# A graph network with two relational layers and two attention layers: attention rows fetched by edge tile and copied to slots by SyncE

## The chip, the cores and the metric

The kernel runs on one core of a Trainium2 chip, in one launch. The metric is the device time of that launch in microseconds (us), the median of several runs. A core has TensorE (PE, matrix products), VectorE (DVE), ScalarE (ACT), GpSimd (POOL) and SyncE (SP, which here only issues transfers), and 16 DMA engines that all of them share.

## The reference, cut to what matters

6250 nodes with 128 features, 100000 edges sorted by their target `dst`. Four layers follow one another, each over all edges: two relational ones (RGCN), then two attention ones (GAT, four heads).

```python
# setup: dst = (6250 * uniform ** 2), then edges sorted by dst
h = relu(layernorm(x))
def _rgcn_layer(h, src, dst, rel, basis, w_comp, loop_w, bias):
    W = einsum('rb,bio->rio', w_comp, basis)
    agg = segment_sum(h[src], dst * 16 + rel)          # per node and relation
    return relu(einsum('nri,rio->no', agg, W) + h @ loop_w + bias)
x = x + rgcn(rgcn(h))
h = relu(layernorm(x))
def _gat(x, src, dst, W, a_src, a_dst, b):             # self loops are added to src, dst
    xw = (x @ W).reshape(n, 4, 32)
    e = leaky_relu(al_s[src] + al_d[dst], 0.2)
    ee = exp(e - segment_max(e, dst)[dst])
    out = segment_sum(ee / den[dst] * xw[src], dst)
    return out + b
h = elu(batchnorm(gat(h))); h = elu(batchnorm(gat(h)))
out = x + h
```

## The kernel before

**Tiles, windows, slots.** The sorted edges are cut into `NG` = 782 tiles of 128 edges. The nodes are cut into 49 windows of 128. A slot is one pair of a tile and a window that it touches: `NGS` = 782 + 48 = 830 slots (832 with padding). A tile that straddles a border between windows has two slots. As `dst` is 6250 times the square of a uniform number, early windows hold many edges and late ones few: tile t lies near window 49 (t/782)^2, so borders are rare at first and come about every eighth tile at the end.

**A layer's loop.** For each slot DVE builds a selection matrix (128 edges x 128 nodes), PE multiplies it with the slot's 128 rows of source features, and DVE adds the product to the window's accumulator in SBUF (`AC`). The source rows come from a table in DRAM by an indirect DMA that POOL issues, one instruction for 128 rows.

- RGCN (`tensor`, `vector`, `scalar`; loops over `s`): POOL gathers the 782 tiles of `Ttab` (one row for each node and relation) into a ring of `TG` = 64 tiles. SP's `relay` waits for each landing and raises `landed[L]` by one. PE reads from registers which tile a slot needs (`TIX`) and where it lies (`OFT`), waits for `landed[L]` to reach that number, and multiplies.
- GAT (`gat_vector`, `gat_scalar`, `gat_tensor`): POOL gathers 830 times, once for each slot, rows of 132 floats of `Gtab` (128 features and 4 attention terms) into a ring of `GR` = 96 slots. Slots are worked in chunks of `CH` = 32. While chunk c is multiplied (L1979) and added (L1128), chunk c+1 is prepared: selections, their transposes, target terms, the maxima by scans, exponentials, and the weights are multiplied into the rows (`weigh`, L1103). In this preparation ACT's copy `als` (L1545) is the first that needs the gathered rows, of all 32 slots.
- A slot's gather in GAT waits for the gather 16 before it and, from slot 96 on, for the product that last read its place.

**Closing.** `NTURN` = 83 turns go over the windows. A turn takes a finished window, weighs it against its self loops (DVE, L588), turns it by two products (PE, L592 and L593), adds the bias (ACT, L1599) and takes statistics for the batch norm (DVE, L1213). `CLOSE` lists batches (slot from which the weights of the batch are worked out, first turn, last turn). Turns 0 to 63 are spread over the slot loop at the places in `PLACES`, the last 19 come after it.

**The start.** SP loads x, `dst` twice (to test that it is sorted), the first parameters, more of x, then `src` and `edge_type`. DVE tests the order (`flag`), PE multiplies the 49 windows by the 16 relation matrices (L1799), and SP stores `Ttab`. Between windows the generators `tables_vector`, `tables_scalar` and `tables_tensor` make the per-slot tables step by step.

Each engine runs its own instruction stream in the order written; counters (semaphores) tie them together.

## Time and profile before

| what | value |
| --- | --- |
| median of 3 runs | 5504.15 us (5494.9 to 5508.55) |
| span of the profiled execution, first to last instruction | 4547.9 us |
| median less span | 956.3 us |
| mean granted TensorE clock | 0.649 of full speed |
| busy share of the span | POOL 69%, PE 69%, DVE 56%, ACT 24% |

The profile covers the span alone; of the profiled execution nothing outside its span is shown. Shares are means over stages with different limits, so they are read by stage.

### The profile page before, as it was taken

The numbers are of one execution on the slowest core, as the hardware profiler recorded it, in microseconds if no ns is written. First come the engines' busy times: TensorE is split into PE (matmuls) and PEld (weight loads), VectorE is DVE, ScalarE is ACT, GpSimd is POOL, SyncE is SP. The second block draws the span as 40 slices with busy tenths as digits, with TensorE's granted clock in tenths as the row PEclk, the third lists the DMA queues.
The fourth block names the chain that finished last, engine by engine and source line by source line (L and its number), as shares of the span: only waits on it lengthen the run. The fifth ranks groups of instructions, "written<-read, shape, count | busy, mean of one in ns | idle before, by whom it ended". The sixth has DMA issues, their size and how long they took to land.

```text
span 4547.9 us, 63220 instructions
## 1 busy us (share of the span) xinstructions
PE 3121.2 (69%) x13439; PEld 2273.6 (50%) x13439; DVE 2544.8 (56%) x9924; ACT 1107.5 (24%) x2623; POOL 3132.4 (69%) x3271
## 2 busy tenths in 40 slices
PE   7976777777756666666646676767674666676766
PEld 3444444444434444444435555656563555565655
DVE  6534444444434455555556566767674667676776
ACT  3311222222200111111122233323332223332333
POOL 1057777777767777777677777777727777777772
PEclk9966889888855555555555566656665556665666
DMA  6633444444432222222222222222212222222222
GB/s 232 259 111 98 151 148 154 149 150 154 154 97 62 65 65 65 66 66 66 61 54 54 54 54 54 54 54 54 54 39 58 55 55 55 55 54 54 54 55 73
DMA packets 168049, 394.03 MB, mean 87 GB/s; under 512 B 57414, under 2 KB 92036, under 8 KB 150532
## 3 DMA queue, kind: packets, MB, share of 16 engines
q0 software_dynamic: 103616, 215.16, 17.9%
q10 hardware_dynamic: 37536, 102.42, 6.0%
q1 hardware_dynamic: 26532, 72.39, 4.3%
q8 instruction: 131, 2.15, 0.2%
q14 instruction: 234, 1.92, 0.1%
HBM read 229.57 MB, written 160.17 MB: 86 GB/s over the span
## 4 chain that ended last, share of the span: by engine, by line
PE 39%; DMA 15%; DVE 14%; issue 13%; POOL 11%; ACT 4%; DVEq 2%; SPq 1%; ACTq 0%; POOLq 0%
DMA Gr<-Ttab,GID 12%; PE B L1837 11%; PE B L1979 8%; POOL Gr L2098 8%; PE B L1737 6%; PE B L1799 3%; POOL Gr L2081 3%; DMA Gr<-Gtab,SRC 3%; DVE XA L1128 2%; DVE XA L935 2%; DVE Sr L1027 2%; PE B L1911 1%; PE B L1895 1%; ACT hold L1534 1%; DVE Gr L1103 1%
## 5 line engine op out<-in xcount | busy, mean ns | idle before, releaser
L2098 POOL DMA_INDIRECT Gr<-Gtab,SRC x1660 | 1603.1, 966 | 584.2 <-issue 448.5
L2081 POOL DMA_INDIRECT Gr<-Ttab,GID x1564 | 1497.3, 957 | 604.6 <-PE B L1837 272.8
L1837 PE MATMUL B<-Gr,Sr 128*128 x3328 | 999.0, 410 | 596.5 <-SPq L2114 328.6
L1837 PEld LDWEIGHTS B<-Gr,Sr 128*128 128x128 f32 x3328 | 731.3, 270 | 1051.9 <-issue 1036.4
L1979 PE MATMUL B<-Gr,Sr 128*128 128x136 f32 x3328 | 959.3, 432 | 132.9 <-DVE XA L1128 80.9
L1979 PEld LDWEIGHTS B<-Gr,Sr 128*128 128x128 f32 x3328 | 740.3, 295 | 203.7 <-DVE XA L1128 130.3
L935 DVE TENSOR_TENSOR XA<-XA,B 128x128 f32 x1664 | 471.6, 283 | 571.8 <-PE B L1837 521.3
L1128 DVE TENSOR_TENSOR XA<-XA,B 128x136 f32 x1664 | 480.8, 289 | 294.2 <-PE B L1979 237.9
L924 DVE TENSOR_SCALAR Sr<-iota,DL 128x128 f32<-128x128 f32 x1664 | 493.3, 300 | 20.6 <-issue 16.2
L1737 PE MATMUL B<-XA,H 128*128 128x512 f32 x664 | 412.5, 709 | 1.7 <-DVE H L602 0.4
L1027 DVE TENSOR_SCALAR Sr<-iota,DL 128x128 f32<-128x128 f32 x1664 | 370.2, 295 | 0.0
L1526 ACT CAST hold<-Sr 128x512 bf16<-128x512 f32 x416 | 257.2, 618 | 431.2 <-DVE Sr L1027 419.3
L1360 ACT COPY Sr<-B 128x512 f32<-128x512 f32 x332 | 194.3, 585 | 470.5 <-PE B L1737 470.5
L1895 PE MATMUL B<-identb,hold 128*128 128x128 bf16 x1664 | 232.3, 286 | 75.0 <-ACT hold L1534 48.6
L1918 PE MATMUL B<-ident,hold 128*128 128x128 f32 x52 | 23.4, 451 | 357.1 <-ACT hold L1545 357.1
L1534 ACT COPY hold<-B 128x512 bf16<-128x512 bf16 x416 | 241.7, 583 | 47.8 <-PE B L1911 45.7
L1103 DVE TENSOR_TENSOR Gr<-Gr,B 128x1024 f32<-128x1024 f32 x202 | 244.6, 1211 | 1.1 <-ACT scs L1579 1.1
L1895 PEld LDWEIGHTS B<-identb,hold 128*128 128x128 bf16 x1664 | 174.8, 132 | 117.4 <-ACT hold L1534 68.2
L1038 DVE TENSOR_TENSOR pen<-hold 128x127 f32<-128x127 f32 x52 | 15.1, 291 | 377.2 <-ACT hold L1549 377.2
L1911 PE MATMUL B<-A,hold 128*128 x1664 | 164.7, 182 | 80.5 <-ACT hold L1534 72.6
L602 DVE COPY H<-B 128x128 f32<-128x128 f32 x215 | 62.0, 289 | 270.2 <-PE B L1715 264.7
L1911 PEld LDWEIGHTS B<-A,hold 128*128 128x128 bf16 x1664 | 142.8, 113 | 123.5 <-issue 105.5
(287 smaller groups left out, 3001.2 us busy)
## 6 DMA issues: line engine op xcount, KB each, us to landing
Ttab<-Sr ACTq DMA_DIRECT2D x83, 1024.0 KB, 4.2
Ttab<-Sr SPq DMA_DIRECT2D x51, 1024.0 KB, 3.9
Gr<-Gtab,SRC POOLq DMA_INDIRECT x1660
Gr<-Ttab,GID POOLq DMA_INDIRECT x1564
Gtab<-Gr ACTq DMA_DIRECT2D x83, 66.0 KB
X1D<-Gr ACTq DMA_DIRECT2D x83, 64.0 KB
out<-Sr SPq DMA_DIRECT2D x12, 256.0 KB
Gtab<-XA SPq DMA_DIRECT2D x5, 528.0 KB, 3.8
```

The source lines that it names most:

```text
L924: e.tensor_scalar(out=selr(sn), in0=iota[:, :], scalar1=DL[:, sn:sn + 1], scalar2=None, op0=ALU.is_equal).then_inc(built_v, 1)
L935: ins = e.tensor_tensor(a, a, B[RGCN_BANKS[L][sa % len(RGCN_BANKS[L])]][:, 0:P], ALU.add)
L1027: e.tensor_scalar(out=sel(s), in0=iota[:, :], scalar1=DL[:, s:s + 1], scalar2=None, op0=ALU.is_equal).then_inc(sel_made, 1)
L1103: e.tensor_tensor(g, g, w, ALU.mult).then_inc(wei_v, 1)
L1128: ins = e.tensor_tensor(a, a, B[s % 3][:, 0:CW], ALU.add)
L1737: e.matmul(B[bk][:, :], hT[:, u % 2, :], wl[1][:, i * 512:(i + 1) * 512], start=True, stop=True).then_inc(row_mm, 1)
L1837: e.matmul(B[banks[s % len(banks)]][:, 0:P], selr(s), Gr[:, bass.ds(o, P)], start=True, stop=True).then_inc(slot_mm, 1)
L1895: mm = e.transpose(bt[:, j * P:(j + 1) * P], sbf[:, g % 2, j * P:(j + 1) * P], identb[:, :])
L1911: mm = e.matmul(B[5][:, 12 * m:12 * m + 12], sts[:, g % 2, j * P:(j + 1) * P], A3[:, bass.ds(off(e, regs[m % 16], 12 * NW), 12)], start=Tr ...
L1979: e.matmul(B[s % 3][:, 0:CW], sel(s), Gr[:, (s % GR) * CW:(s % GR + 1) * CW], start=True, stop=True).then_inc(gat_mm, 1)
L2081: e.indirect_dma_start(out=Gr[:, (sn + 1) % TG * P:((sn + 1) % TG + 1) * P], out_offset=None, in_=Tt[L][:, :], in_offset=bass.IndirectOffs ...
L2098: e.indirect_dma_start(out=Gr[:, (s % GR) * CW:(s % GR) * CW + 132], out_offset=None, in_=T2[L][0:NPAD][:, :], in_offset=bass.IndirectOffs ...
```

## The change

1. **GAT by tiles.** POOL gathers 782 tiles a layer, not 830 slots, into a new ring of 64 tiles behind `Gr`, whose slot ring shrinks from 96 to 64. POOL announces landed tiles in fours: before it issues the last tile of a four, it waits for the four before and raises `landed[2 + L]` by 4. From tile 16 on a gather waits for the copy of the slot 16 before it (`spread`).
2. **Slot copies.** SP runs `to_slots`: for each slot it waits until its tile has landed and its place is free, and copies 128 x 132 floats from the tile ring to the slot ring, SBUF to SBUF. What waited for gathers in GAT (ACT's `als`, DVE's clearing of `AC`) now waits for copies.
3. **Source table.** `SRC` is no longer selected for each slot by 28 products and two copies, but made for each tile by one shift of `GID` on DVE.
4. **A fifth batch** in `CLOSE`: turns 64 to 71 move into the slot loop, 11 stay behind it.
5. **First loads.** `dst` comes before x; `src` and `edge_type` before most of x; the later parts of x and the second basis wait until the first relation matrices have been loaded. DVE tests the order before it measures x. Tables start at window 3, not 1. Loads of 112 rows are cut into 96, 15 and 1.
6. **Landing counts.** The number that PE (and now SP) waits for is first bounded below by 1 with a register instruction.

Arrays are placed anew in SBUF to make room; the arithmetic of the layers is the same.

```diff
-GR = 96
+GR = 64
+TW = 132
+TQ = 4
+NTQ = 8
-CLOSE = ((239, 0, 17), (399, 17, 34), (558, 34, 52), (668, 52, 64))
+CLOSE = ((239, 0, 17), (399, 17, 34), (558, 34, 52), (668, 52, 64), (736, 64, 72))
+        def wait_tiles(e, L, g):
+            e.wait_ge(tiles[L][g % NTQ], 16 * TQ * (g // NTQ) + 16 * min(TQ, NG - TQ * g))
+        def wait_spread(e, n):
+            e.wait_ge(spread[n % NSG], 16 * (n // NSG + 1))
...
+            then(e.tensor_scalar(out=SRC[:, :], in0=GID[:, 0:NT], scalar1=4, scalar2=None, op0=ALU.arith_shift_right), "src")
...
-                if w >= 1 and not early:
+                if w >= LATER and not early:
...
-                for n in range(n0 + NSG, min(n0 + 2 * NSG, 2 * NG + (L + 1) * NGS)):
-                    wait_gather(e, n)
+                for n in range(end - NSG, end):
+                    wait_spread(e, n)
                 then(e.copy(v3(dc[:, 1, :]), G3(c, 128, 132).rearrange("p s h -> p h s")), "als")
...
-                        e.wait_ge(landed[L], kregs[s % 32 // 16][s % 16])
+                        e.reg_alu(kreg, kregs[s % 32 // 16][s % 16], 1, ALU.max)
+                        e.wait_ge(landed[L], kreg)
...
-                for s in range(NGS):
-                    n = 2 * NG + L * NGS + s
-                    wait_gather(e, n - NSG)
-                    if s >= GR:
-                        e.wait_ge(gat_mm, L * NS + s - GR + 1)
+                for t in range(NG):
+                    g = t // TQ
+                    if t % TQ == TQ - 1 and g:
+                        wait_tiles(e, L, g - 1)
+                        e.sem_inc(landed[2 + L], TQ)
+                    back = t - TG + NGS - NG
+                    if back >= 0:
+                        wait_spread(e, L * NGS + back)
                     e.indirect_dma_start(
-                        out=Gr[:, (s % GR) * CW:(s % GR) * CW + 132], out_offset=None, in_=T2[L][0:NPAD][:, :],
-                        in_offset=bass.IndirectOffsetOnAxis(ap=SRC[:, s:s + 1], axis=0)).then_inc(gat[n % NSG], 16)
+                        out=TILES[:, (t + 1) % TG * TW:((t + 1) % TG + 1) * TW], out_offset=None, in_=T2[L][0:NPAD][:, :],
+                        in_offset=bass.IndirectOffsetOnAxis(ap=SRC[:, t:t + 1], axis=0)).then_inc(tiles[L][g % NTQ], 16)
+                for g in range((NG + 1) // TQ - 1, -(-NG // TQ)):
+                    wait_tiles(e, L, g)
+                    e.sem_inc(landed[2 + L], TQ)
...
+        def to_slots(e, L, kreg, kregs, oregs):
+            for s in range(NGS):
+                n = L * NGS + s
+                if s % 16 == 0:
+                    e.reg_load(kregs, TIX[:, s:s + 16])
+                    e.reg_load(oregs, OFT[0:1, s:s + 16])
+                if n >= NSG:
+                    wait_spread(e, n - NSG)
+                if s >= GR:
+                    e.wait_ge(gat_mm, L * NS + s - GR + 1)
+                e.reg_alu(kreg, kregs[s % 16], 1, ALU.max)
+                e.wait_ge(landed[2 + L], kreg)
+                o = off(e, oregs[s % 16], (TG - 1) * TW)
+                e.dma_start(Gr[:, s % GR * CW:s % GR * CW + TW], TILES[:, bass.ds(o, TW)]).then_inc(spread[n % NSG], 16)
...
-            x_load(0)
             for k, (t, o) in enumerate(((fdi, 0), (fni, 1))):
                 e.wait_ge(ready, k + 1)
                 flat_load(t, "dst", o, flat_dst)
+            x_load(0)
+            for k, (t, name) in enumerate(((fsi, "src"), (fri, "edge_type_16"))):
+                e.wait_ge(ready, k + 3)
+                flat_load(t, name, 0, flat_sem)
             e.dma_start(lw[0][:, :], I["L0_gnn_loop_w1"]).then_inc(first_params, 16)
             e.dma_start(rb[0][:, :], row(I["L0_gnn_bias1"])).then_inc(first_params, 16)
+            e.wait_ge(wall_sem[0], 16)
             x_load(1)
             x_load(2)
```

POOL's queue in GAT, before: gathers of slots 94 to 97 of the first GAT layer, where the second wait comes in.

```order
L2098 DMA Gr<-Gtab,SRC 128x132 [waits gather10]
L2098 DMA Gr<-Gtab,SRC 128x132 [waits gather11]
L2098 DMA Gr<-Gtab,SRC 128x132 [waits gat_products,gather12]
L2098 DMA Gr<-Gtab,SRC 128x132 [waits gat_products,gather13]
L2098 DMA Gr<-Gtab,SRC 128x132 [waits gat_products,gather14]
```

And of the change: the first gathers of the same layer, by tile.

```order
L2122 DMA Gr<-Gtab,SRC 128x132 [waits tables_vector,rest_done]
L2122 DMA Gr<-Gtab,SRC 128x132 x6
L2122 DMA Gr<-Gtab,SRC 128x132 [waits tiles0_0]
L2122 DMA Gr<-Gtab,SRC 128x132 x3
L2122 DMA Gr<-Gtab,SRC 128x132 [waits tiles0_1]
L2122 DMA Gr<-Gtab,SRC 128x132 x3
L2122 DMA Gr<-Gtab,SRC 128x132 [waits tiles0_2]
L2122 DMA Gr<-Gtab,SRC 128x132 [waits spread0]
L2122 DMA Gr<-Gtab,SRC 128x132 [waits spread1]
L2122 DMA Gr<-Gtab,SRC 128x132 [waits spread2]
```

POOL no longer waits for products; every fourth gather waits for the four tiles before its own four, and from tile 16 on each waits for a slot copy.

SP's queue between the relational and the attention layers had nothing to do for GAT but the stores of the second table. In the change it holds three rows for each of 1660 slots; here from slot 63 of the first GAT layer, where the wait for products comes in (L2159 is the copy).

```order
L2156 REGISTER_ALU [waits spread15]
L351 ISA [waits landed2]
L2159 DMA Gr<-Gr 128x132
L2150 TENSOR_LOAD TIL
L2151 TENSOR_LOAD TIL
L2156 REGISTER_ALU [waits gat_products,spread0]
L351 ISA [waits landed2]
```

What POOL waited for before (the product that frees a place) now stands ahead of SP's copy, 64 slots back.

SP's queue at the start of the program, before.

```order
L2125 DMA XA<-in_x 128x16x128
L2121 DMA Gr<-in_dst 111x896 [waits cleared]
L2122 DMA Gr<-in_dst 1x544
L2121 DMA Gr<-in_dst 111x896 [waits cleared]
L2122 DMA Gr<-in_dst 1x543
L2130 DMA lw<-in_L_gnn_loop_w 128x128
L2131 DMA rb<-in_L_gnn_bias 128x128
L2125 DMA XA<-in_x 128x16x128 x2
```

The same place in the change.

```order
L2167 DMA Gr<-in_dst 96x896 [waits cleared]
L2168 DMA Gr<-in_dst 15x896
L2169 DMA Gr<-in_dst 1x544
...
L2169 DMA Gr<-in_dst 1x543
L2172 DMA XA<-in_x 128x16x128
...
L2180 DMA lw<-in_L_gnn_loop_w 128x128
L2181 DMA rb<-in_L_gnn_bias 128x128
L2172 DMA XA<-in_x 128x16x128 [waits wall0]
```

The first part of x moved behind `dst`, and its second and third parts behind the load of the relation matrices.

## Rows read from the trace of the kernel before

**Rows 1.** Groups by line: busy us, mean ns, then idle time before and what ended it.

```profile
L2098 POOL DMA_INDIRECT Gr<-Gtab,SRC x1660 | 1603.1, 966 | 584.2 <-issue 448.5 <-PE B L1979 122.5 <-DVEq L973 13.3
L1837 PE MATMUL B<-Gr,Sr 128*128 x3328 | 999.0, 410 | 596.5 <-SPq L2114 328.6 <-DVE XA L935 222.1 <-issue 40.5
```

**Rows 2.** Timeline of POOL: start, duration, idle before; relational, then attention layer.

```profile
261.66 0.98 POOL L2081 DMA_INDIRECT Gr<-Ttab,GID  x1 [0.30 <-issue]
...
2425.92 0.95 POOL L2098 DMA_INDIRECT Gr<-Gtab,SRC  x1 [0.30 <-issue]
```

**Rows 3.** Stretches of three layers: PE, PEld, DVE, ACT, POOL, clock, DMA share, GB/s.

```profile
400.00:1240.00 840.00, 630.97 (x2287) 378.36 (x2287) 354.68 (x1578) 209.43 (x396) 637.01 (x666) 0.86 0.44 151
...
2280.00:3320.00 1040.00, 692.53 (x3811) 583.35 (x3812) 678.38 (x2525) 315.55 (x779) 791.60 (x816) 0.59 0.21 54
3430.00:4460.00 1030.00, 694.90 (x3846) 583.29 (x3846) 680.89 (x2526) 316.89 (x783) 781.95 (x815) 0.60 0.21 55
```

**Rows 4.** Waits in a chunk with closing, 3183 to 3223 us: total, times, longest.

```profile
ACT hold L1545 <- DMA Gr<-Gtab,SRC: 7.0, 1, 7.0
```

**Rows 5.** Timeline, end of the first GAT layer's gathers and what follows.

```profile
3329.95 0.95 POOL L2098 DMA_INDIRECT Gr<-Gtab,SRC  x1 [0.30 <-issue]
3333.32 0.42 ACT L1545 COPY hold<-Gr 128x128 f32<-128x128 f32 x1 [8.08 <-DMA Gr<-Gtab,SRC]
...
3344.27 4.45 PE L1979 MATMUL B<-Gr,Sr 128*128 128x136 f32 x18
```

**Rows 6.** Transfers of 66 KB like a slot copy: issue on ACT, and time to landing.

```profile
L1399 ACTq MOVE Gtab<-Gr x83: 29/29/29, 1406.5 to 2268.9; - x83
L1399 ACTq DMA_DIRECT2D Gtab<-Gr x83: 338/338/339, 1406.6 to 2268.9; - x83
DMA to landing us min/median/max: 3.4/3.9/5.0
```

**Rows 7.** Timeline of SP at the start: issue of two loads of 1 MB of x.

```profile
12.02 14.91 SPq L2125 DMA_DIRECT2D XA<-in_x  x2
```

**Rows 8.** Timeline of DVE after the last slot of the first GAT layer: first and last of 19 turns.

```profile
3372.00 1.10 DVE L588 TENSOR_TENSOR Gr<-XA,GID 128x256 f32 x3 [0.25 <-DVE GID L1187]
...
3386.28 0.29 DVE L1213 BATCH_NORM_STATS2 XA<-XA  x1 [0.23 <-ACT XA L1599]
```

**Rows 9.** Busy time in two stretches of these turns; granted clock third from last.

```profile
3372.00:3377.00 5.00, 4.52 (x21) 4.52 (x22) 3.34 (x11) 1.47 (x4) 0.00 (x0) 0.50 0.00 0
3378.00:3386.00 8.00, 7.56 (x52) 6.41 (x50) 7.09 (x25) 4.83 (x14) 0.00 (x0) 1.00 0.00 0
```

**Rows 10.** Timeline of the start: order test, its branch, matrices loaded, first window's products.

```profile
17.04 0.33 ACTq L1419 DMA_DIRECT2D Wrel<-Sr  x1
...
25.05 0.82 ACTq L1438 DMA_DIRECT2D XA<-Wrel  x1
...
26.81 0.63 DVE L865 CAST Gr<-Gr 112x896 f32<-112x896 int32 x1 [6.18 <-DMA Gr<-in_dst]
...
30.50 0.15 DVE L872 CAST flag<-B 1x1 int32<-1x1 f32 x1 [0.28 <-PE B L1776]
36.12 0.49 DVE L602 COPY H<-B 128x128 f32<-128x128 f32 x2 [5.48 <-issue]
...
36.47 5.17 PE L1799 MATMUL B<-XA,H 128*128 128x512 f32 x8 [5.39 <-DVE H L602]
```

**Rows 11.** Transfers: line, count, KB, us from issue to landing.

```profile
Wrel<-Sr ACTq DMA_DIRECT2D x4, 512.0 KB, 5.7
XA<-Wrel ACTq DMA_DIRECT2D x1, 0.5 KB, 11.1
XA<-Wrel SPq DMA_DIRECT2D x1, 0.5 KB, 7.9
```

**Rows 12.** Instruction fetches during the span: packets, MB.

```profile
q8 instruction: 131, 2.15, 0.2%
q14 instruction: 234, 1.92, 0.1%
```

More of the change, by code:

```diff
@@ L154, in build @@
         H = sb("H", [P, 4, P])
-        lw = [sb(f"lw{l}", [P, P]) for l in range(2)]
+        lwp = [sb(f"lw{l}", [P, P + (1 if l == 0 else 0)]) for l in range(2)]
+        lw, pen = [x[:, 0:P] for x in lwp], lwp[0][:, 0:129]
         rb = [sb(f"rb{l}", [P, P]) for l in range(2)]
@@ L209, in build @@
         built_v = sem("selection_made")
-        landed = [sem(f"landed{l}") for l in range(2)]
+        landed = [sem(f"landed{l}") for l in range(4)]
+        tiles = [[sem(f"tiles{l}_{i}") for i in range(NTQ)] for l in range(2)]
+        spread = [sem(f"spread{i}") for i in range(NSG)]
         slot_mm, slot_add = sem("slot_products"), sem("slot_added")
@@ L243, in build @@
         FB, MM, zz, dc = (hold[:, 1024 + 256 * k:1280 + 256 * k].rearrange("p (i e) -> p i e", i=2) for k in range(4))
-        dx = hold[:, 2048:2304]
-        penF, penL, ads = (hold[:, 2304 + 128 * k:2432 + 128 * k] for k in range(3))
+        dx = DST[:, 0:256]
+        penF, penL, ads = (DST[:, 256 + 128 * k:384 + 128 * k] for k in range(3))
+        CONT, PBK, PFK = ROWS[0:1, :], ROWS[32:33, 0:NS], ROWS[64:65, 0:NS]
+        PBR, PFR = XW[0:1, 4096:4096 + NS], XW[0:1, 4096 + NS:4096 + 2 * NS]
+        TILES = Gr[:, GR * CW:GR * CW + TG * TW]
         rl = Gr[:, NPAD:NPAD + 2048].rearrange("p (i j e) -> p i j e", i=2, j=2)
@@ L298, in build @@
         a3w = A3[:, :].rearrange("p (w k h) -> p w k h", k=3, h=4)
-        art = [ar[:, k, :].rearrange("p (w h) -> p w h", h=4) for k in range(2)]
+        art = [GID[:, k * 4 * NW:(k + 1) * 4 * NW].bitcast(f32).rearrange("p (w h) -> p w h", h=4) for k in range(2)]
         OT = Gr[:, 0:NPAD]
@@ L740, in tables_vector @@
             yield "early"
-            for _ in range(5):
+            e.wait_ge(ta.sem, ta.at("gid1"))
+            then(e.tensor_scalar(out=SRC[:, :], in0=GID[:, 0:NT], scalar1=4, scalar2=None, op0=ALU.arith_shift_right), "src")
+            for _ in range(3):
                 yield
@@ L828, in vector, with weights_of @@
             e.wait_ge(mixv.sem, mixv.at("mkh"))
-            for l in range(2):
-                w3 = (hn[:, 0, :], pen[:, 0:P])[l].rearrange("p (r b) -> p r b", b=NBAS)
+            def weights_of(l):
+                w3 = (hn[:, 0, :], wc[:, 1, :])[l].rearrange("p (r b) -> p r b", b=NBAS)
                 e.wait_ge(mix_par[l], 32)
@@ L857, in scale @@
                 e.scalar_tensor_tensor(out=nb[:, sl], in0=mv[:, sl, 0], scalar=-1.0, in1=rstd[:, sl], op0=ALU.mult, op1=ALU.mult).then_inc(scaled, 1)
-            for w in range(AHEAD):
-                measure(w)
-            variance(0)
-            scale(0)
-            e.wait_ge(flat_dst, 64)
+            e.wait_ge(flat_dst, 96)
             flagv.done(e.tensor_copy(dF, fdi), "dF")
@@ L870, in vector @@
             flagv.done(e.tensor_reduce(out=small[:, 0:1], in_=lF, axis=AX, op=ALU.add), "sum")
+            for w in range(AHEAD):
+                measure(w)
+            variance(0)
+            scale(0)
             e.wait_ge(flagp, 1)
@@ L979, in vector @@
             e.memset(A3[:, :], 0.0).then_inc(late, 1)
+            e.tensor_scalar(out=OFT, in0=OFT, scalar1=TW / P, scalar2=None, op0=ALU.mult).then_inc(late, 1)
             for L in range(2):
@@ L990, in gat_vector @@
             if L == 0:
-                e.wait_ge(late, 5)
+                e.wait_ge(late, 6)
             else:
@@ L1405, in scalar, with basis_load @@
             aregs, dregs = registers(e, "aturn", 8), registers(e, "arows", 8)
-            for l in range(2):
+            def basis_load(l):
                 n = str(l + 1)
@@ L1459, in scalar @@
                     mixed(1, w - 8)
-                if w >= 1 and not early:
+                if w >= LATER and not early:
                     early = next(tables) == "early"
@@ L1501, in gat_scalar @@
             if L == 0:
-                e.wait_ge(late, 5)
+                e.wait_ge(late, 6)
             def prep(c):
@@ L1506, in prep @@
                 c0 = c * CH
-                n0 = 2 * NG + L * NGS + c0
+                end = (L * NGS) + min(c0 + CH, NGS)
                 def then(ins, name):
@@ L1807, in tensor @@
                     mix(1, w - 8)
-                if w >= 1 and not early:
+                if w >= LATER and not early:
                     early = next(tables) == "early"
@@ L2159, in sync @@
             rest(e, rest2_store, "r2s")
+            e.wait_ge(rest_done, 2)
+            e.wait_ge(late, 6)
+            to_slots(e, 0, kreg, kregs, oregs)
             for w0, w1 in STORED:
```

118 lines of the change are left out of this document (60 added, 58 removed).

## The prediction

> **What bounds the kernel now.** I read the groups by line first, then POOL's timeline, then busy time by stage, then the waits inside single chunks. POOL has the largest single entries: 1660 GAT gathers of 966 ns, with 448.5 us of gaps put down to nothing but the issue [rows 1]. Its timeline shows the same thing everywhere: a gather of about 0.95 us, a gap of 0.30 us, the next gather [rows 2]. The gap is 0.30 us whether the instruction waits for nothing (the first row) or for two semaphores (the second), so it belongs to the issue and isn't a wait, though some of it is put down to PE by name. By stage this gives 840/666 = 1.261 us a gather in the first relational layer, 1040/816 = 1.275 and 1030/815 = 1.264 in the two GAT layers [rows 3]. No other engine is full: in the GAT stretches DVE is busy 65% and PE 67% at a granted clock of 0.59 and 0.60. The waits inside a chunk say who is ahead: ACT's `als` stands 7.0 us for gathered rows even in a chunk where turns are closed beside it [rows 4]. The product units wait for POOL, and POOL for nobody. So from the first gather on, time is the number of gathers times 1.26 us, plus the short pieces between layers in which POOL rests. That is the term the change touches.
>
> **Part 1 and 3, fewer gathers.** 830 - 782 = 48 gathers fall away in each GAT layer. 48 x 1.275 + 48 x 1.264 = 61.2 + 60.7 = **-121.9 us**. The work that took the source table for each slot lay in the relational loop, where PE waits 328.6 us for landings [rows 1]; taking it away is worth 0, since POOL sets the pace there.
>
> Does the gain hold where it arises? It arises late: borders come about every eighth tile at the end (98/782 a tile), so a chunk of 32 slots needs 32/1.125 = 28.4 gathers and lasts 28.4 x 1.264 = 35.9 us, against 32 x 1.264 = 40.4 now. The other engines need 40.4 - 7.0 = 33.4 us for a closing chunk [rows 4]. So POOL still ends last, by 2.5 us. The fifth batch puts its weights and eight turns into chunks that had none; they then look like the closing chunk that I have just used.
>
> Does the price of a gather stay? POOL gets one wait and one counter step for every four gathers. Waits add nothing to the gap of 0.30 us [rows 2]; the step costs at most a register move of 29 ns [rows 6]: 392 x 0.029 = 11 us at most, 0 at least. I take 0, since the gap swallowed two waits as well. For traffic, the first layer's gathers went at 1.261 us with the DMA engines at 0.44, and GAT has 0.21 [rows 3]. A copy moves as many bytes as a gather, so at most another 0.21 comes on top: 0.42, below what was harmless.
>
> **Part 2, can SP keep up?** It must make 830 copies while POOL makes 782 gathers: one in 782 x 1.264 / 830 = 1.19 us. An issue of 66 KB by registers took 0.338 us on ACT's queue, and a register move 0.029 us [rows 6]; with three such steps that is 0.43 us. The dear bound is SP's own queue when it was choked: 14.91 us for two loads of 16 x 128 rows of 512 bytes, so 4096 pieces, 3.6 ns each, 0.47 us for 128 [rows 7]. Both are far below 1.19. Copies overlap, since sixteen may be under way: at 5.0 us to landing, the worst of 83 [rows 6], that is one in 0.31 us. I take no cost for the pace.
>
> In the same place the Trainium skill ("DMA: Bandwidth & Descriptors", "Rules for kernel authors" and "Anatomy of one DMA") speaks against transfers this small: under 64 KB one pays mostly overhead, and a transfer (measured there for POOL's) costs about 2.0 us plus its bytes at 436 GB/s. By that a copy of 68 KB would take an estimated 2.2 us, not the 3.9 us of the row, and the sum below would be 3 us lower; 830 of them one behind the other would outlast a layer, which the sixteen counters prevent.
>
> **Do the rings stall?** A gather waits for the copy of the slot 16 before it, 16 x 1.264 = 20.2 us earlier. The first tile of a four is announced when POOL reaches the seventh gather after it (8.5 us), SP issues up to four copies (1.9), and they land in 3.9: 14.3 us, or 15.4 at the worst landing. It fits with 5 us to spare. POOL's wait for the four tiles before wants a landing within 4 x 1.264 - 0.30 = 4.8 us of the issue; the last gather of a layer let ACT go after 3333.32 - 3329.95 = 3.37 us [rows 5]. Free. The slot ring shrinks from three chunks to two, but `als` goes 11 us before the next chunk's products begin (3333.32, 3344.27 [rows 5]), so a chunk is multiplied well within the two chunks that its places have.
>
> **What the detour costs.** It adds latency, which a layer pays once, at its end; at its beginning POOL isn't held up. After the last gather nothing lags (its landing is announced at once), but SP then issues three or four copies and the last must land: 3 x 0.43 + 3.9 = 5.2, up to 1.9 + 5.0 = 6.9, at least 3.4. I take 5.5. It isn't hidden: ACT had stood 8.08 us at that place, waiting for just this [rows 5]. Twice: **+11 us**.
>
> **Part 4.** After the last slot 19 turns a layer (83 less the 64 in `CLOSE`) run one behind the other, from 3372.00 to 3386.57: 14.6 us, 0.77 a turn [rows 8]. The clock is granted at 0.50 (1.2 GHz) at first and at 1.00 (2.4 GHz) later [rows 9], so what is left may be the slow ones: I take 0.69 instead of 0.77 for eight, 5.5 us. Twice: **-11 us** (5 to 7 each). In the slot loop the eight turns lie under `als`'s waiting: 8.08 us there without turns [rows 5], 7.0 with them [rows 4].
>
> **Part 5, the start.** The first window's product waited until 36.47 us for two things together: the order test (`dst` landed at 26.81, flag 30.50, branch until 36.12) and the matrices (issued 25.05, 11.1 us to landing, so 36.15) [rows 10, 11]. Before the test DVE had measured x, and had been done by 26.81 - 6.18 = 20.6. With `dst` first, the test's 3.7 us come ahead of that work: flag at 24.3, branch over at 29.9 at the latest. The matrices are then late: their store's second half is issued at 17.04 as before, lands after 5.7 at the median, and the load takes 7.9 as its uncrowded twin did [rows 10, 11]: 17.0 + 5.7 + 0.8 + 7.9 = 31.4, 5.1 us earlier than 36.5. But the second part of x is issued only then, and DVE wants it one window (5.2 us) later, while a load of its size takes 7.9: 2.7 lost. Net **-2.4 us** (between -10, if all was crowding, and +3).
>
> **Part 6.** One register step more for each of 1664 relational slots, 0.029 us each [rows 6], 48 us in all on PE's queue, under PE's 328.6 us of waiting for landings [rows 1]: 0; 48 if that cover were gone.
>
> **Sum.** -121.9 + 11 - 11 - 2.4 = -124.3. The profiled span of 4547.9 becomes 4424. The median lies 956.3 us above the span, and I carry that over: 5504.15 - 124.3 = **5380 us**.
>
> **Rivals.**
> - *Late chunks meet the other engines.* If copies arriving in fours and a busier DVE cost a late chunk more than the 2.5 us to spare, the chunks of the last third run at, say, 40 us as now. Half of the borders lie there: about 60 us of the gain go, 5440. Against it: the 7.0 us of wait in a closing chunk [rows 4]. For it: it is the thinnest margin.
> - *POOL stops for tiles (the slow side).* If the copies, which share the engines with the gathers, stretch a gather's landing beyond 4.8 us, POOL stops at every fourth. A landing of L costs (L - 4.8) x 391 us over both layers. At 5.1 us all of the gain is gone, at 5.5 the time is 5380 + 274 = 5654. Against it: 3.37 us at a DMA share of 0.21 [rows 3, 5]. The Trainium skill's section "Issuing engines are not separate DMA queues" says that transfers of all engines interleave on the same 16; it gives no size.
> - *SP sets the pace.* Above 1.19 us a copy the layer follows SP; each 0.1 us costs 166, so at 1.27 nothing is left, and at 1.4 the kernel is slower: 5380 + 0.21 x 1660 = 5729. Against it: 0.34 and 0.47 us [rows 6, 7].
> - *What lies outside the span grows with the program.* The change adds about 6900 instructions to 63220, 11%; if the 956 us were in proportion, 104 would come on top: 5484. Against it: the fetches inside the span, 2.15 + 1.92 = 4.07 MB, are 64 bytes for each instruction [rows 12], so the program is loaded while it runs.
>
> **How the numbers follow.** My forecast 0.74, with a range of its own of 5355 to 5400 (start -10 to +3, ends 3.4 to 6.9, POOL's steps 0 to 11, and the runs' own spread of 14 us). Late chunks 0.12, POOL stops 0.06, SP 0.04, outside 0.04. The range reaches into the late-chunk case: 5352 to 5430. A change of under 0.3% (16 us) couldn't be told from none. Faster: 0.74 + 0.12 + 0.04 = 0.90; the rest is slower 0.08, same 0.02.
>
> **What the new profile would show.** POOL with 782 gathers in each GAT layer, still at 0.95 + 0.30 us: the gap tells of stops. ACT's wait at `als` shorter by some 4 us in late chunks than in early ones, but not gone. SP's copies issued in fours with rests between. About 9 us from a layer's last gather to `als`, where it was 3.37. Eleven turns at the end. The first product of a window at about 31 us. I would be wrong above all if POOL's gaps grow at every fourth gather, or if `als` no longer waits late in a layer.

## The result, and the profile after

| | median us | runs |
|---|---|---|
| before | 5499.89 | 4 (5494.90 to 5508.55) |
| after | 5587.65 | 4 (5571.52 to 5591.39) |

Ratio 1.0154, 95% interval 1.014 to 1.0167: **slower by 88 us**, 1.5% and clear of the noise, where 124 us less was forecast.

From the page of the changed kernel: its span, its chain, and its two kinds of gathers (the line is now L2122 in the GAT layers, L2100 in the relational ones):

```profile
span 5586.9 us, 68766 instructions
...
PE 24%; issue 18%; another core or an unknown queue 17%; DVE 12%; ACT 5%; DVEq 2%; POOL 1%; SPq 1%; DMA 1%; ACTq 0%; POOLq 0%
...
L2122 POOL DMA_INDIRECT Gr<-Gtab,SRC x1564 | 1513.9, 968 | 1134.1 <-DMA Gr<-Gr 552.2
L2100 POOL DMA_INDIRECT Gr<-Ttab,GID x1564 | 1502.0, 960 | 996.6 <-issue 393.6
```

Two things stand out. The profiled execution took 5588.66 us, so its span of 5586.9 leaves 1.8 us outside. The profile of before had 956 us between its span and the median; they can't have been a fixed cost around the span. And a gather takes 968 ns, where it was 966 [rows 1], but POOL idles 1134 us between the GAT gathers where it was 584, and as much between the relational ones, which the change leaves alone.

POOL's and the other engines' timeline of the changed kernel in the first relational layer (start, us, engine, line, tiles, count, idle time before and what ended it):

```profile
623.13 0.38 PE L1856 MATMUL B<-Gr,Sr 128*128 x2
...
625.17 0.29 DVE L955 TENSOR_TENSOR XA<-XA,B 128x128 f32 x1 [5.17 <-remote]
625.79 0.96 POOL L2100 DMA_INDIRECT Gr<-Ttab,GID  x1 [1.70 <-remote]
626.48 1.07 ACT L1376 COPY Sr<-B 128x512 f32<-128x512 f32 x2 [4.36 <-remote]
...
631.76 1.64 PE L1856 MATMUL B<-Gr,Sr 128*128 x6 [3.42 <-issue]
```

DVE's addition needs the product that ended at 623.51, and begins 1.66 us later; ACT's eviction begins later still; "remote" says that the trace holds no event that would have let them go. In [rows 2] POOL stood 0.30 us before each gather and never 1.70. POOL's and DVE's queues were both let go at 625.06, 1.5 us after that product. I call these gaps halts. They come at waits of every engine, mostly 1 to 5 us long, in the slot loops of all four layers. So the profile of before and the runs that it stood beside were of two conditions, and the experiments met both. On three chips the kernel before takes 4556 to 4562 us (the span of its profile was 4547.9), on a fourth 5502 us, like the 5500 us above, whose chip isn't on record. Each experiment is compared with the kernel before on its own chip. As each chip was met in one set of runs only, it isn't shown whether the condition belongs to the chip or to the time.

### The profile page after: what moved, and what is told of

Read it like the earlier page. It is cut to its first block, busy times and chain, and to the rows that moved or that the text cites. A ratio compares the mean times of both kernels' runs of the same rounds, so it can differ in the third digit from the quotient of the medians.

```text
span 5586.9 us, 68766 instructions
## 1 busy us (share of the span) xinstructions
PE 3147.8 (56%) x13411; PEld 2324.0 (42%) x13411; DVE 2560.3 (46%) x9945; ACT 1122.0 (20%) x2623; POOL 3047.5 (55%) x3175
## 4 chain that ended last, share of the span: by engine, by line
PE 24%; issue 18%; another core or an unknown queue 17%; DVE 12%; ACT 5%; DVEq 2%; POOL 1%; SPq 1%; DMA 1%; ACTq 0%; POOLq 0%
PE B L1998 7%; PE B L1856 6%; PE B L1754 3%; DVE XA L1149 2%; DVE XA L955 2%; PE B L1914 2%; ACT hold L1552 2%; PE B L1930 2%; DVE Sr L944 1%; DVE Sr L1048 1%; POOL Gr L2100 1%; ACT hold L1544 1%; DVE Gr L1124 1%; PE B L608 1%
## 5 line engine op out<-in xcount | busy, mean ns | idle before, releaser
L2122 POOL DMA_INDIRECT Gr<-Gtab,SRC x1564 | 1513.9, 968 | 1134.1 <-DMA Gr<-Gr 552.2
L2100 POOL DMA_INDIRECT Gr<-Ttab,GID x1564 | 1502.0, 960 | 996.6 <-issue 393.6
L1856 PE MATMUL B<-Gr,Sr 128*128 x3328 | 886.6, 396 | 741.0 <-issue 372.7
L1998 PE MATMUL B<-Gr,Sr 128*128 128x136 f32 x3328 | 1016.8, 444 | 393.8 <-issue 176.3
L1914 PE MATMUL B<-identb,hold 128*128 128x128 bf16 x1664 | 246.1, 300 | 433.4 <-ACT hold L1552 272.3
L1754 PE MATMUL B<-XA,H 128*128 128x512 f32 x664 | 455.0, 775 | 58.9 <-issue 35.2
L1817 PE MATMUL B<-XA,H 128*128 128x512 f32 x392 | 179.8, 602 | 3.5 <-DVE H L618 3.5
L1754 PEld LDWEIGHTS B<-XA,H 128*128 128x128 f32 x664 | 132.2, 247 | 81.2 <-issue 43.9
```

The costliest lines, as they stand in the source:

```text
L1754: e.matmul(B[bk][:, :], hT[:, u % 2, :], wl[1][:, i * 512:(i + 1) * 512], start=True, stop=True).then_inc(row_mm, 1)
L1856: e.matmul(B[banks[s % len(banks)]][:, 0:P], selr(s), Gr[:, bass.ds(o, P)], start=True, stop=True).then_inc(slot_mm, 1)
L1914: mm = e.transpose(bt[:, j * P:(j + 1) * P], sbf[:, g % 2, j * P:(j + 1) * P], identb[:, :])
L1998: e.matmul(B[s % 3][:, 0:CW], sel(s), Gr[:, (s % GR) * CW:(s % GR + 1) * CW], start=True, stop=True).then_inc(gat_mm, 1)
L2100: e.indirect_dma_start(out=Gr[:, (sn + 1) % TG * P:((sn + 1) % TG + 1) * P], out_offset=None, in_=Tt[L][:, :], in_offset=bass.IndirectOffs ...
L2122: e.indirect_dma_start(out=TILES[:, (t + 1) % TG * TW:((t + 1) % TG + 1) * TW], out_offset=None, in_=T2[L][0:NPAD][:, :], in_offset=bass.I ...
```

## The experiments

**Single parts, on a chip where before takes 4562.42 us.** The register step of part 6 alone, once and twice:

```diff
-                        e.wait_ge(landed[L], kregs[s % 32 // 16][s % 16])
+                        e.reg_alu(kreg, kregs[s % 32 // 16][s % 16], 1, ALU.max)
+                        e.wait_ge(landed[L], kreg)
```

> The kernel before with part 6 alone: one register step (max with 1) ahead of each of 1664 waits of PE in the relational layers. Theory A (the step costs, or it is the bounded wait that changes the pace of the relational layers): 1.01 to 1.03 times before, and a span near 5550 us. Theory B (the loss is in attention by tiles with SP's copies): 1.000 within 0.003, 5500 us. On the span: if the profile of the kernel before showed the same execution as its timed runs, the span here is about 4550 with a time of 5500; if the timed runs have stalls that that profile lacks, the span is about 5500 and a gather's pace in the first relational layer is 1.5 us, as in the changed kernel, not 1.26.

> The kernel before with part 6 and a second register step behind the first. Theory A: as much again on top of the run with one step, 1.02 to 1.06 times before. Theory B: 1.000 within 0.003, like the run with one step, since PE waits for landings anyway.

Measured 4562.06 us (ratio 0.9999, 0.9989 to 1.0008) and 4562.95 (1.0002, 0.9992 to 1.0012). The step is free, and the kernel with one step stands for the kernel before from here on. Its span is 4560.0 of 4561.92 us.

The fifth batch alone, then the reordered first loads alone, each on top of that:

```diff
-CLOSE = ((239, 0, 17), (399, 17, 34), (558, 34, 52), (668, 52, 64))
+CLOSE = ((239, 0, 17), (399, 17, 34), (558, 34, 52), (668, 52, 64), (736, 64, 72))
```

> The kernel before with the fifth closing batch (part 4), and part 6, which the attention layers don't see. If the terms of the prediction hold, 11 us (10 to 14) less than the run with part 6 alone, ratio 0.998 to it. Rival: the eight turns inside the slot loop cost there what they save at its end: no difference, or some us more.

```diff
-            x_load(0)
             for k, (t, o) in enumerate(((fdi, 0), (fni, 1))):
                 e.wait_ge(ready, k + 1)
                 flat_load(t, "dst", o, flat_dst)
+            x_load(0)
...
+            e.wait_ge(wall_sem[0], 16)
             x_load(1)
```

> The kernel before with the reordered first loads, tables from window 3 (part 5), and part 6. If the term of the prediction holds, 2.4 us less (10 less to 3 more) than the run with part 6 alone, and the first product of a window at about 31 us. Rival: the later tables or the late x hold up the first gather: 5 us or more slower.

The fifth batch alone: 4550.42 us (0.9977, 0.9967 to 0.9987), 12 us less. The first loads, with all the rest of part 5: 4556.93 us (0.9990, 0.9981 to 1.0000), 5.5 us less, which is at the edge of the noise; in the profiles the first gather of all comes 5.3 us earlier (256.48 against 261.74).

**The whole change and its tiles, on a second chip (before 4555.84 us).** The changed kernel as it is:

> The changed kernel once more, on a chip on which the kernel before took 4562 us in the runs so far, as its profile shows it, and not 5500. Theory A, that the loss of 1.5% belongs to the condition of the runs with long halts in it: here the sum of the prediction holds, minus 124 us (4438 us, ratio 0.973, with 0.967 to 0.984 allowed), the gathers of both GAT layers keep the pace of before (1.27 us each) and no engine stands still for reasons that the trace does not name. Theory B, that attention by tiles is slower by itself: 1.5% slower here too (4630 us), the pace of a gather in the GAT layers above 1.36 us, with POOL waiting for tiles or SyncE's copies at more than 1.4 us each.

Measured **4442.29 us, ratio 0.9751 (0.9738 to 0.9765)**: faster by 113.5 us. Theory A holds. Without parts 4 and 5 (the loads stay cut in three):

```diff
-CLOSE = (..., (668, 52, 64), (736, 64, 72))
-LATER = 3
+CLOSE = (..., (668, 52, 64))
+LATER = 1
```

> Attention by tiles alone, with four closing batches and the old order of the first loads. By the sum of the prediction minus 111 us against the kernel before (96 gathers fewer at 1.27 us, plus 11 us of latency at the ends of the two layers), 4451 us, ratio 0.976. Theory B: slower than before, ratio above 1.01. The difference to the whole change should be the 12 and 5.5 us that the fifth batch and the first loads gave alone, 17 us in all.

Measured 4438.31 us, 0.9742 (0.9727 to 0.9756): 117.5 us less, where 111 was expected. But the whole change isn't 17 us better than its tiles, it is 4 us behind them. The end of the first GAT layer shows why. First ACT's `als` copies of the kernel before (L1545), then those of the whole change (L1563), for the last five chunks:

```profile
3181.56 0.42 ACT L1545 COPY hold<-Gr 128x128 f32<-128x128 f32 x1 [6.20 <-DMA Gr<-Gtab,SRC]
3223.04 0.42 ACT L1545 COPY hold<-Gr 128x128 f32<-128x128 f32 x1 [7.51 <-DMA Gr<-Gtab,SRC]
3263.70 0.42 ACT L1545 COPY hold<-Gr 128x128 f32<-128x128 f32 x1 [3.66 <-DMA Gr<-Gtab,SRC]
3304.26 0.42 ACT L1545 COPY hold<-Gr 128x128 f32<-128x128 f32 x1 [7.28 <-DMA Gr<-Gtab,SRC]
3343.50 0.42 ACT L1545 COPY hold<-Gr 128x128 f32<-128x128 f32 x1 [8.87 <-DMA Gr<-Gtab,SRC]
```

```profile
3129.75 0.43 ACT L1563 COPY hold<-Gr 128x128 f32<-128x128 f32 x1
3167.76 0.42 ACT L1563 COPY hold<-Gr 128x128 f32<-128x128 f32 x1 [3.79 <-DMA Gr<-Gr]
3204.99 0.42 ACT L1563 COPY hold<-Gr 128x128 f32<-128x128 f32 x1
3240.73 0.42 ACT L1563 COPY hold<-Gr 128x128 f32<-128x128 f32 x1
3281.91 0.42 ACT L1563 COPY hold<-Gr 128x128 f32<-128x128 f32 x1
```

Before, `als` waited for gathered rows in each chunk (2.6 to 10.7 us in the last eight). Now it waits in one of the last five. That is not the fifth batch's doing alone: with tiles alone six of the last eight copies of the second layer don't wait either. But the chunks from 3204.99 to 3281.91 last 35.7 and 41.2 us, and `als` waits at the end of neither, so the last one, with the fifth batch in it, is 41 us long by the engines' own work. With the fifth batch alone, on the kernel before, that chunk was 38.3 us long and `als` still waited, by a hair:

```profile
3296.88 0.42 ACT L1544 COPY hold<-Gr 128x128 f32<-128x128 f32 x1 [6.66 <-DMA Gr<-Gtab,SRC]
3335.18 0.42 ACT L1544 COPY hold<-Gr 128x128 f32<-128x128 f32 x1 [0.60 <-DMA Gr<-Gtab,SRC]
```

In the whole change POOL issued its last gather of the layer long before `als`:

```profile
3263.06 0.95 POOL L2122 DMA_INDIRECT Gr<-Gtab,SRC  x1 [0.30 <-issue]
3264.32 0.99 POOL L2122 DMA_INDIRECT Gr<-Gtab,SRC  x1 [0.30 <-issue]
3265.61 1.01 POOL L2122 DMA_INDIRECT Gr<-Gtab,SRC  x1 [0.30 <-issue]
```

From the last gather to `als` it is 16.3 us, where it was 3.4 [rows 5]. With tiles alone it is 6.2 us, and `als` still waits for the copies:

```profile
3273.86 1.01 POOL L2122 DMA_INDIRECT Gr<-Gtab,SRC  x1 [0.30 <-issue]
```

```profile
3280.06 0.43 ACT L1563 COPY hold<-Gr 128x128 f32<-128x128 f32 x1 [0.52 <-DMA Gr<-Gr]
```

**Tiles announced in eights and in twos, same chip.** `TQ = 4` becomes 8 or 2.

> The changed kernel, but tiles are announced in eights in place of fours. A group of eight is announced only after the next eight gathers are issued, so up to 15 of the 16 tile slots are held by tiles that SyncE may not copy yet. By the prediction's reading of the ring (14.3 to 15.4 of 20.2 us are used at fours), the loop from a gather over its announcement, copy and landing back to its slot grows by some 10 us above the 20.2 us that 16 gathers last: POOL then stops, by 4 to 6 us per 16 gathers and 780 gathers of each layer, 400 to 600 us in all. If the ring is not what limits (Theory B in the form that single copies are too slow), the time is that of the changed kernel within 20 us.

> The changed kernel, but tiles are announced in pairs. The loop of the ring gets 5 us shorter, the end of each layer some 2 us earlier, and POOL issues twice as many announcements (390 a layer). If the ring has its 5 us of slack at fours, no difference but the 4 us at the layer ends (minus 0 to 6 us); if the ring is tight at fours already, faster by tens of us.

Eights: 4452.77 us (0.9776, 0.9761 to 0.9791), 10 us more than fours and not 400. My expectation was wrong for two reasons. The wait is for the copy of the slot 16 before, and that slot's tile lies the further back the more borders have passed: only the first chunks have no more than 16 tiles of room. And there POOL kept its 0.30 us as well, because the announcement doesn't wait for the gathers that are written ahead of it in POOL's queue. These rows are the 8th, the 10th and the 16th gather of the first GAT layer, with SyncE's first eight copies between them:

```profile
2277.75 0.95 POOL L2122 DMA_INDIRECT Gr<-Gtab,SRC  x1 [0.30 <-issue]
...
2280.27 0.95 POOL L2122 DMA_INDIRECT Gr<-Gtab,SRC  x1 [0.30 <-issue]
2280.79 5.76 SPq L2159 DMA_DIRECT2D Gr<-Gr  x8
...
2287.92 1.29 POOL L2122 DMA_INDIRECT Gr<-Gtab,SRC  x1 [0.31 <-issue]
```

The first eight tiles are announced ahead of the 16th gather in POOL's queue, yet the first copy starts at 2280.79, 3.0 us after the eighth gather and 7.1 us before the 16th. Over the layer a group was announced 2.6 us at the median after its last gather began, with eights, 2.7 with fours: as soon as it had landed, while gathers ahead of the announcement in POOL's queue were still to run. What eights cost lies at the layer's end (20.2 us from the last gather to `als`).

Twos: **5234.30 us (1.1487, 1.147 to 1.1505)**, 792 us more than fours, where I had expected at most 6 us less. This is POOL's timeline with twos:

```profile
2999.55 0.95 POOL L2122 DMA_INDIRECT Gr<-Gtab,SRC  x1 [1.26 <-DMA Gr<-Gtab,SRC]
3000.81 1.13 POOL L2122 DMA_INDIRECT Gr<-Gtab,SRC  x1 [0.30 <-issue]
3003.11 0.95 POOL L2122 DMA_INDIRECT Gr<-Gtab,SRC  x1 [1.17 <-DMA Gr<-Gtab,SRC]
3004.37 0.95 POOL L2122 DMA_INDIRECT Gr<-Gtab,SRC  x1 [0.31 <-issue]
```

The gather of 3003.11 stands behind the announcement of the one of 2999.55 and begins 3.56 us after it: the landing is seen some 2.7 us after the issue (the median of the announcements with twos), and the announcement and the start of the next gather take the rest. Two gathers without a stop would take 2 x 1.264 = 2.53 us. So each pair stops for 1.03 us, and 782 pairs in the two layers make about the 792 us. With fours four gathers, 5.06 us, pass over the same 3.56. So the rival "POOL stops for tiles" was a real edge, crossed at twos and kept clear by 1.5 us at fours.

**The condition of 5502 us.** A third set of runs met it. The kernel before, for the profile that was missing:

> The kernel before with its landing counts bounded, one look, for its profile on the chip of this job. If the chip is in the condition of 4560 us, the profile shown of before returns. If it is in the condition of 5500 us, this is the profile that was missing: by Theory A (the halts of some us come at random times to waits of every engine) the two RGCN layers take 170 us each more than in the profile of before, the GAT layers 150 to 200 us each more, by gaps of 1 to 6 us before instructions with a wait.

Measured 5495.43 us, one run. From its page:

```profile
span 5493.5 us, 63220 instructions
...
PE 34%; another core or an unknown queue 24%; issue 17%; DVE 13%; ACT 5%; POOL 2%; DVEq 2%; DMA 2%; SPq 1%; ACTq 0%; POOLq 0%
...
L2100 POOL DMA_INDIRECT Gr<-Gtab,SRC x1660 | 1600.8, 964 | 1047.5 <-issue 486.4
L2083 POOL DMA_INDIRECT Gr<-Ttab,GID x1564 | 1497.7, 958 | 1007.0 <-issue 427.6
```

Beside it the same kernel on a chip without halts:

```profile
span 4560.0 us, 63220 instructions
...
PE 35%; POOL 18%; DMA 15%; issue 14%; DVE 13%; ACT 4%; DVEq 2%; ACTq 0%; POOLq 0%; SPq 0%
...
L2100 POOL DMA_INDIRECT Gr<-Gtab,SRC x1660 | 1608.5, 969 | 583.6 <-issue 454.2
L2083 POOL DMA_INDIRECT Gr<-Ttab,GID x1564 | 1501.1, 960 | 606.7 <-issue 250.7
```

The same gathers take the same time; only what lies between them has grown. From a layer's first gather to its last it is 182 and 158 us more in the relational layers, as expected, and 202 and 211 us more in the GAT layers, above the 150 to 200. In the chain, POOL's 18% and its transfers' 15% have shrunk to 2% and 2%: **with halts the gathers no longer set the pace**, the engines' handing over to one another does. The changed kernel without its fifth batch, same chip:

> The changed kernel without the fifth closing batch (tiles and reordered loads). Read from the runs so far: tiles alone took 4438.3 us, the whole change 4442.3 us, and the first loads alone saved 5.5 us, so with tiles the fifth batch must cost some 9 us that it saves without them (Theory A: with 48 gathers fewer a layer the engines end behind the gathers, and the blocks of the fifth batch stand in their way). Expected 4433 us, ratio 0.973, and the copy of als at the end of the first GAT layer 2 to 5 us earlier against the layer's first gather than in the whole change. Theory B: the 4 us between the two are scatter and the fifth batch gives its 12 us here as before: 4454 us without it.

Measured 5569.48 us, 1.0132 (1.0113 to 1.0151). Its expectation was written for the other condition, and its Theory A is answered below. And the kernel before with useless copies on SyncE in the GAT layers:

```diff
+            for s in range(NGS):
+                wait_gather(e, 2 * NG + L * NGS + s)
+                for m in range(2):
+                    ...
+                    e.dma_start(waste[n % 4 * P:(n % 4 + 1) * P, :], ident[:, :]).then_inc(wasted[n % 4], 16)
```

> The kernel before, in whose two GAT layers SyncE waits for each gather and then issues two useless copies of 64 KB to DRAM, 3320 in all, so that more completion events and small packets pass than the changed kernel's 1660 copies make. If that traffic by itself were what made the changed kernel slow in the condition of 5500 us (it has 96 thousand recorded semaphore events where the kernel before has 77 thousand), halts should show here: tens to hundreds of us more. If the traffic is free, 4560 us as before within 10 us. I expect the second, with 3 to 1.

Measured 5544.30 us, 1.0073 (1.0056 to 1.009): 43 us more. I had expected nothing. Useless copies alone don't make the 68 us that tiles and loads cost here, but they aren't free.

**Load on VectorE, on a chip without halts (before 4555.90 us).** If it is the engines' pace that takes the gain away, a busier engine must do so on any chip. Both kernels get one more instruction a slot:

```diff
+                if L or s:
+                    e.wait_ge(more, L * NS + s)
+                e.tensor_reduce(out=spare[:, :], in_=iota[:, :].unsqueeze(1).to_broadcast([P, 4, P]), axis=AX, op=ALU.add).then_inc(more, 1)
                 ins = e.tensor_tensor(a, a, B[s % 3][:, 0:CW], ALU.add)
```

> The kernel before with one more reduction of 128x512 on VectorE (about 0.55 us by its number of columns) ahead of each slot's addition in both GAT layers, 1664 in all; its result is not used. VectorE then has about 1.45 us of work a slot, against the 1.27 us of a gather, so that the layers are paced by the engines, as the traces show them to be in the condition of 5500 us. Expected on a chip of 4560 us: 200 to 350 us more, 4830 us.

> Tiles and reordered loads with the same reduction before each slot's addition. Theory A (tiles save gathers, and gathers alone; where the engines set the pace there is nothing to save, and the detour over SyncE is left as a cost): within 25 us of the kernel before with the same reductions, not 120 us below it. Theory B (the loss on the other chip is of its halts alone, in POOL's waits for landed tiles): here, without halts, tiles still gain some 100 us against the kernel before with the same load.

Measured 4853.67 us (ratio 1.0653, 1.0637 to 1.067) and 4860.64 us (1.0665, 1.0649 to 1.0682). **The 118 us that tiles and loads gain elsewhere are gone.** Between the two medians are 7 us the other way, and the intervals overlap. POOL's last gather of the first GAT layer and `als` behind it, with tiles and load:

```profile
3350.90 0.95 POOL L2128 DMA_INDIRECT Gr<-Gtab,SRC  x1 [0.30 <-issue]
```

```profile
3459.52 0.30 ACT L1562 COPY hold<-DL 128x128 f32<-128x128 f32 x1
3459.85 0.29 ACT L1565 COPY PF<-ROWS 1x128 f32<-1x128 f32 x1
3460.17 0.30 ACT L1566 COPY PB<-ROWS 1x128 f32<-1x128 f32 x1
3460.49 0.43 ACT L1569 COPY hold<-Gr 128x128 f32<-128x128 f32 x1
```

`als` comes 110 us after the last gather and waits for nothing but ACT's own copies. On the same chip:

> The changed kernel without its fifth closing batch, once more, since its first run met the condition in which the kernel before takes 5500 us. If this chip gives the kernel before 4555 to 4562 us: 4433 us, ratio 0.973 (0.971 to 0.975), that is at least as fast as the whole change and tiles alone. If it is again the condition of 5500 us: ratio 1.013 as before.

> The kernel before with 3320 useless copies of 64 KB, two for each gather of the GAT layers. They cost 43 us in the condition of 5500 us. On a chip without halts: nothing, within 10 us, if completion events and packets are dear only where the events halt; 40 us again if it is the copies' own traffic or their interleaving with the gathers' packets.

Tiles and loads without the fifth batch: **4437.43 us, 0.9742 (0.9729 to 0.9755)**, against 0.9751 (0.9738 to 0.9765) for the whole change. The intervals overlap, so with tiles the fifth batch doesn't give its 12 us; whether it costs the difference of 5 is left to the rows: the last `als` of the first GAT layer comes 11.9 us earlier after the first gather than in the whole change, for 2 to 5 expected, and 4.5 us of that are lost again before the next layer's first gather. The idle copies: 4554.98 us, 0.9997 (0.9987 to 1.0006), free on a chip without halts.

All of it in one table, in us, for the first GAT layer, worked out from the starts of POOL's first and last gather and of the last `als` in each trace:

| kernel | halts | first to last gather | last gather to `als` | first gather to `als` | `als` to next layer's gather |
|---|---|---|---|---|---|
| before (bounded counts) | no | 1061.3 | 3.4 | 1064.6 | 81.9 |
| fifth batch alone | no | 1058.7 | 3.4 | 1062.0 | 76.4 |
| tiles alone | no | 999.3 | 6.2 | 1005.5 | 82.9 |
| tiles and loads | no | 996.1 | 6.3 | 1002.4 | 80.7 |
| whole change | no | 998.0 | 16.3 | 1014.3 | 76.2 |
| before, more VectorE | no | 1122.7 | 61.8 | 1184.5 | 106.1 |
| tiles, more VectorE | no | 1081.7 | 109.6 | 1191.3 | 105.1 |
| before | yes | 1263.4 | 42.7 | 1306.1 | 83.9 |
| before, idle copies | yes | 1287.6 | 45.0 | 1332.6 | 83.7 |
| tiles and loads | yes | 1256.1 | 84.8 | 1340.9 | 83.3 |
| whole change | yes | 1272.8 | 95.3 | 1368.2 | 77.5 |

The last column hardly knows the halts: between the layers they cost 1 to 3 us. Nor does the start: from the first instruction to the first gather of all it is 261.7 us in the kernel before without halts and 260.4 with them.

## Why the prediction was wrong

**The step that failed is the last line of the sum**: "The median lies 956.3 us above the span, and I carry that over". Nothing lies above the span (1.8 us here, 1.9 in the kernel before on either kind of chip). In the condition of 5502 us the kernel before has a span of 5493.5 us in a run of 5495.43. So the 956 us were halts within the span, which the profile shown was free of, and they changed what bounds the GAT layers: there tiles and loads cost 68 us instead of gaining 118. "Time is the number of gathers times 1.26 us" held for the profile and not for the runs. I had one rival about these 956 us, and it asked whether they grow with the program's size; that they might lie between the instructions, so that POOL no longer leads, I didn't ask. (It also took the growth too high: the change adds 68766 - 63220 = 5546 instructions, not 6900.)

Where the profile's condition holds, the sum came out 11 us too good: -124.3 forecast, -113.5 measured, and part of that nearness is luck, since three terms missed by 3 to 20 us in opposite ways. By its terms, in that condition:

- **Fewer gathers, -121.9.** With tiles alone the gathers of the two layers last 61.9 and 59.9 us less (999.3 against 1061.3, 991.0 against 1050.9): -121.8. Right, and POOL's gap stayed 0.30 us. But the cover I read for it was thin. I took the 7.0 us of one chunk for every closing chunk, and the waits of the last eight copies go down to 2.6 us. With tiles alone most late `als` copies wait for nothing, against the sign that I had named ("shorter ... but not gone"). POOL still never stopped, as the rings took up the chunks that ran late.
- **The detour, +11.** From the last gather to `als` 6.2 us in place of 3.4, and 6.7 in place of 3.3 in the second layer: +6. The place was right, the landing of a copy was too dear at the 3.9 us of a row for DRAM. With tiles and loads SyncE's eleven last copies are issued by 3263.69 + 9.48 = 3273.17, each issue taking 0.51 us, so the last from 3272.66 on, and `als` begins at 3274.61: 1.95 us. That is near the estimate of 2.2 us by the Trainium skill ("DMA: Bandwidth & Descriptors", "Anatomy of one DMA"), and its sum, 3 us below mine, was the better one in this term.

```profile
3263.69 9.48 SPq L2160 DMA_DIRECT2D Gr<-Gr  x11
```

- **The fifth batch, -11.** Right alone (-12), wrong in company. With tiles it moves `als` 10 us back and gives 7 back after it: +3.4 us for the first layer (92.5 us from last to next gather against 89.1) and +5.8 at the second's end (92.7 against 86.9). Against tiles with loads it is +5.5 and +2.8, the same 8 to 9 us in all. The step that failed here is "in the slot loop the eight turns lie under `als`'s waiting", with "POOL still ends last, by 2.5 us" behind it. I took 33.4 us for a closing chunk's work; the fifth batch's chunk takes 38.3 - 0.6 = 37.7 us of it in the run with that batch alone (39.6 - 1.9 in the second layer, the same), less than the 40.4 us of 32 gathers and more than the 35.9 us of a late chunk with tiles. Rival 1, late chunks that meet the other engines, was right in kind: some 10 us a layer at `als`, in the batch's chunk, not 60.
- **The start, -2.4.** -5.5 alone; in the whole change the first gather comes 4.8 us earlier. The first window's product came at 31.27 us, for a forecast of 31.4; of the 2.7 us that I gave back for x nothing shows.
- **SP's pace, POOL's steps, the register step: 0.** Right, with less room than I said. An issue alone took 507 ns on SP at the median; I had estimated 0.43 us with its three register steps. With them it is 0.75 us, from the eight copies in 5.76 us shown above. Against 1.19 that still suffices.

```profile
L2159 SPq DMA_DIRECT2D Gr<-Gr x1660: 506/507/1897, 2274.6 to 4353.3; - x185
```

In the condition of the timed runs the same table reads otherwise. Between the kernel before and tiles with loads, the gathers of the layer end only 7 us earlier in place of 65 (62 with tiles alone), since POOL must wait for places that the engines free late (274 us for copies in that layer's waits of the changed kernel), and `als` comes 34.8 us later. What tiles add on paths that the engines set is shown by the VectorE pair: +6.8 us a layer. More copies cost there too: 1660 useless ones in the layer moved `als` by 26.5 us, so 830 would be an estimated 13 in proportion. These make 20 of the 35. The last 15 us a layer stay open: a path over two more queues, each wait of which may be halted, would explain them, but no run takes it apart. One place where the traces show more time is SyncE's own queue: 663 of its register steps and waits took over 0.3 us in the halted trace of the changed kernel, up to 1.6 us, and none in the other. The fifth batch, whose turns stand in the way of busy engines, is most of the rest: 5587.65 against 5569.48 us without it, though from two sets of runs.

What the halts are isn't settled either. Shown is what they aren't. The engines' instructions and the DMA packets last as long as elsewhere (a gather's last packet ends 2.2 us after its issue at the median in both traces of the changed kernel). And the longer gaps fall before instructions with a wait: of 448 gaps on PE that are over 1 us longer than in the same kernel's other trace all are at a wait, and on DVE 500 of 502, though only 46% and 69% of these engines' instructions have one. That speaks against an engine that is slow by itself or lacks its code; it doesn't tell a halted wait from one for an engine that was halted.

Where they fall says more. The trace also keeps fewer semaphore events, 34841 where the other one has 96480. In the start both traces have the same 2339 events, 9 a us, and the start takes no longer. In the slot loops the one without halts has 18 to 28 a us and the halted one 3.5 to 7. So halts and lost events come together, in the stretches where events are dense, and tiles raise that density in GAT from 17 to 27 a us. Events that are delivered late would fit that; so would a recording that can't keep up with them and holds the engines, and every span here comes from such a recording. Neither was tested.

## What to carry to other kernels

Set the profiled execution's own span against the timed runs before anything else: if they differ by more than a few us, the profile is of another condition, the difference is not a constant to be added, and the bound must be read anew, or the forecast widened to both signs. A saving on the engine that leads is worth only the lead that it has: here 48 gathers a layer were worth 61 us where POOL led, and less than nothing where the others did. Read that lead from the tightest chunk and not from one: it was 2.6 us where I had read 7.0. And two edits that live on the same slack (fewer gathers, turns under the wait for gathers) must be costed together, since the first takes away the cover of the second.

## What the runs showed of the hardware

- The same program took 4556 to 4562 us on three chips and 5502 on a fourth, 20% more, steadily (5494.57 to 5503.38 in seven runs), with unchanged durations of the engines' instructions and of packets. The added time lies in the slot loops; the start (261.7 and 260.4 us to the first gather) is the same.
- Useless copies on an idle queue, 3320 of 64 KB, cost 0 us (0.9987 to 1.0006) on one chip and 43 us on the halted one.
- A gather's last packet ends 2.2 us after the issue's start, POOL's announcement of it comes after 2.7, and the first instruction that needed it began after 3.4 (ACT's copy) and 3.56 us (POOL's next gather, with twos). A ring that is announced on landing must allow for the last.
- A wait and a counter step that are written between POOL's gathers aren't held back by gathers ahead of them that have yet to run: with eights the announcement was raised 7.5 us at the median before the gather that it precedes began.
- A reduction of 128x512 took 677 ns on DVE, for 0.55 us that I had estimated by columns.
